# Decoder layer on one core: the first four attention steps between single products of the last two down tiles instead of behind whole tiles from the seventh on

## The reference

```python
x = x + attn(layernorm(x))            # 16 query heads, 2 key heads, head size 32, RoPE, causal
x = x + mamba(ctx, layernorm(x))      # state-space block: 16 states, a scan over 512 positions, gated by z
x = x + moe_ffn(layernorm(x))         # gate/up/down with DFF = 1408, 8 LoRA experts, the best 2 used
```

## Time and profile before

| what | value |
|---|---|
| median of 3 runs | 1439.26 us |
| the profiled execution's own time | 1439.63 us |
| its span | 1437.8 us |
| PE busy | 1290.9 us, 90% |
| DVE busy | 1026.8 us, 71% |
| ACT busy | 676.2 us, 47% |
| mean granted TensorE clock | 0.93 |

### The profile page before, as it was taken

One profiled execution on the slowest core, in us unless ns is written; L12 is line 12 of the kernel. 1 busy time (PEld: TensorE's weight loads), 2 busy tenths in 40 slices (PEclk: granted clock), 3 DMA queues, 4 the chain that ended last, 5 costly groups with the idle time before them and its releaser, 6 DMA issues.

```text
span 1437.8 us, 15860 instructions
## 1 busy us (share of the span) xinstructions
PE 1290.9 (90%) x5680; PEld 627.8 (44%) x5680; DVE 1026.8 (71%) x1238; ACT 676.2 (47%) x1465; POOL 89.0 (6%) x116
## 2 busy tenths in 40 slices
PE   5767778899998899899999799899999799799999
PEld 2334444444443465444444365444444365344443
DVE  5799996889899565789999574788899564521110
ACT  5356553365552395465543286365552287121110
POOL 0000001100000000010000000100000000100000
PEclk8856558999999899999999899999999899799999
DMA  6276662147777410147777410137777311011111
GB/s 233 56 179 152 149 136 56 46 126 186 186 198 170 118 31 1 45 112 186 186 196 168 106 44 20 45 91 188 186 188 178 83 58 31 15 38 55 55 59 54
DMA packets 53196, 158.50 MB, mean 110 GB/s; under 512 B 4992, under 2 KB 10880, under 8 KB 44672
## 3 DMA queue, kind: packets, MB, share of 16 engines
q0 software_dynamic: 9216, 67.11, 23.4%
q1 hardware_dynamic: 25520, 54.01, 11.4%
q10 hardware_dynamic: 18384, 36.37, 8.6%
HBM read 85.91 MB, written 4.46 MB: 63 GB/s over the span
## 4 chain that ended last, share of the span: by engine, by line
PE 61%; DVE 25%; ACT 7%; issue 4%; DMA 2%; ACTq 0%; POOL 0%; DVEq 0%
PE ps_a L920 20%; PE ps_a L934 10%; DVE state L1129 9%; PE ps_a L1005 6%; PE ps_b L945 5%; DVE state L1124 4%; PE ps_w L899 4%; PE ps_a L836 3%; ACT r L618 3%; DVE state L1134 3%; PE ps_b L853 2%; DVE neg_max L1165 2%; PE ps_a L968 2%; PE ps_w L868 2%; DMA y_sb<-state 1%
## 5 line engine op out<-in xcount | busy, mean ns | idle before, releaser
L920 PE MATMUL ps_a<-xt,w_sb 128*128 128x512 f32 x704 | 311.7, 595 | 0.0
L1129 DVE TENSOR_TENSOR_SCAN state<-decay,state 128x2048 f32<-128x2048 f32 (+1 forms) x82 | 284.4, 3478 | 2.5 <-ACT decay L584 0.6
L920 PEld LDWEIGHTS ps_a<-xt,w_sb 128*128 128x128 f32 x704 | 133.2, 191 | 170.0 <-issue 170.0
L682 ACT ACTIVATE r<-ps_a 128x512 f32<-128x512 f32 x132 | 78.5, 597 | 255.2 <-PE ps_a L934 139.1
L1307 DVE TENSOR_TENSOR r<-r,ps_a 128x512 f32<-128x512 f32 x132 | 90.0, 684 | 135.6 <-ACT r L682 135.6
L934 PE MATMUL ps_a<-r,wb_sb 128*128 128x512 f32 x352 | 165.6, 593 | 6.5 <-DVE r L1307 6.5
L584 ACT ACTIVATE decay<-dt_sb,decay_rate 128x511 f32<-128x511 f32 x256 | 163.0, 710 | 5.6 <-DVE state L1129 5.2
L618 ACT ACTIVATE r<-ps_a,neg_max 128x384 f32<-128x384 f32 (+3 forms) x224 | 121.6, 562 | 62.9 <-DVE neg_max L1165 56.8
L1134 DVE TENSOR_TENSOR state<-state,bc_sb 128x2048 f32<-128x2048 f32 (+1 forms) x73 | 147.6, 2022 | 1.6
L1124 DVE TENSOR_TENSOR state<-du_sb,bc_sb 128x2048 f32<-128x2048 f32 x64 | 146.2, 2284 | 1.5 <-DMA bc_sb<-bc_rows 0.9
L853 PE MATMUL ps_b<-cst,r 128*128 128x128 f32 x640 | 108.4, 307 | 25.8 <-ACT r L630 11.5
(11 more groups left out here) (137 smaller groups left out, 1419.5 us busy)
## 6 DMA issues: line engine op xcount, KB each, us to landing
y_sb<-state POOLq DMA_DIRECT2D x64, 1024.0 KB, 9.3
bc_sb<-bc_rows ACTq DMA_DIRECT2D x64, 512.0 KB, 5.9
w_sb<-in_w_tiles SPq DMA_DIRECT2D x44, 512.0 KB, 8.6
w_sb<-in_w_down SPq DMA_DIRECT2D x28, 256.0 KB, 4.2
wb_sb<-in_w_adapt SPq DMA_DIRECT2D x44, 128.0 KB, 2.1
xa<-in_x SPq DMA_DIRECT2D x4, 1024.0 KB, 5.4
wd_sb<-in_w_down SPq DMA_DIRECT2D x16, 256.0 KB, 7.3
out_x<-xb SPq DMA_DIRECT2D x16, 256.0 KB, 2.0
```

Source lines behind the costliest of these rows:

```text
L920: mm = nc.tensor.matmul(ps_a[:, 2 * (f % 2) + half, :], w_sb[:, slot, at + k * P:at + (k + 1) * P], xt[:, k, :], start=(k == 0), stop=Fals ...
L1129: done(nc.vector.tensor_tensor_scan(flat, decay[:, n % 2, tiles, :].rearrange("p j l -> p (j l)"), flat, 0.0, ALU.mult, ALU.add))
```

## The change

The early steps leave their places behind whole tiles. On PE they stand in a table `EARLY_AT` with places (f, i), "behind product i of tile f". Scores 0 come behind product 1 of tile 9, scores 1 behind product 2; in tile 10 transposes 0 stand behind product 1, transposes 1 behind product 2, scores 2 behind product 3; scores 3 stand behind the first closing product (place (FT, 0)). Tiles 7 and 8 follow tile 6 with nothing between. ACT does exponents 0 and 1 in slot 7, both moves in slot 8, exponents 2 and 3 in slots 9 and 10. DVE does maxima 0 and 1 in slot 7, behind that slot's scan piece, the inverses of 0 and 1 in slot 8 behind its piece, maxima 2 and 3 in slots 9 and 10; the inverse of 2 goes behind the residual additions, ahead of maxima 4. In batch 0 PE's order stays the same; those of ACT and DVE change as in the others.

```diff
-SCORES_AT = {FT - 5: 0, FT - 4: 1, FT - 2: 2, FT - 1: 3}
-TURNS_AT = {FT - 3: 0, FT - 2: 1}
+EARLY_AT = {(FT - 2, 1): ("scores", 0), (FT - 2, 2): ("scores", 1), (FT - 1, 1): ("turn", 0), (FT - 1, 2): ("turn", 1),
+            (FT - 1, 3): ("scores", 2), (FT, 0): ("scores", 3)}
...
             def early_steps(b, f):
-                if f in TURNS_AT:
-                    move_transposed(b, TURNS_AT[f])
-                if f in SCORES_AT:
-                    exponents(b, SCORES_AT[f])
+                if f == FT - 4:
+                    exponents(b, 0)
+                    exponents(b, 1)
+                elif f == FT - 3:
+                    move_transposed(b, 0)
+                    move_transposed(b, 1)
+                elif f >= FT - 2:
+                    exponents(b, f - FT + 4)
...
-            def early_steps(b, f):
-                if f in TURNS_AT:
-                    transpose_probs(b, TURNS_AT[f])
-                if f in SCORES_AT:
-                    scores(b, SCORES_AT[f])
+            def early_steps(b, place):
+                kind, s = EARLY_AT.get(place, (None, None))
+                if kind == "scores":
+                    scores(b, s)
+                elif kind == "turn":
+                    transpose_probs(b, s)
...
                         mm = nc.tensor.matmul(ps_a[:, i, :], hb[:, f, i * P:(i + 1) * P], wd_ring[slot],
                                               start=(f == 0), stop=False, skip_group_check=True)
+                        if b is not None and i < NT - 1:
+                            early_steps(b, (f, i))
                     mm.then_inc(wd_used, 1)
                     if b is not None:
+                        early_steps(b, (f, NT - 1))
                         project(b, f)
-                        early_steps(b, f)
                 pe.wait_ge(down_ready, t + 1)
                 for i in range(NT):
                     nc.tensor.matmul(ps_a[:, i, :], down_low[:, i * P:(i + 1) * P], bd_sb[:],
                                      start=False, stop=True, skip_group_check=True).then_inc(out_full, 1)
+                    if b is not None:
+                        early_steps(b, (FT, i))
...
                 project(0, f)
-                early_steps(0, f)
+            for place in EARLY_AT:
+                early_steps(0, place)
...
             def early_steps(b, f):
-                if f in SCORES_AT:
-                    s = SCORES_AT[f]
-                    maxima(b, s)
-                    if s >= 1:
-                        invert_sums(b, s - 1)
+                if f == FT - 4:
+                    maxima(b, 0)
+                    maxima(b, 1)
+                elif f == FT - 3:
+                    invert_sums(b, 0)
+                    invert_sums(b, 1)
+                elif f >= FT - 2:
+                    maxima(b, f - FT + 4)
...
                 for s in range(STEPS + 4):
+                    if s == EARLY:
+                        invert_sums(b, s - 2)
                     if EARLY <= s < STEPS:
                         maxima(b, s)
```

## The result

The changed kernel took 1405.37 us (median of 4, 1403.74 to 1408.29) for 1439.05 before (4 runs measured beside it); the ratio is 0.9768 with a 95% interval of 0.9748 to 0.9788. Two more sets of runs gave 0.9781 (0.9766 to 0.9795) and 0.9784 (0.9770 to 0.9799); one run of the kernel before beside the last set took 1570.17 us at a granted clock of 0.81 and is left out of it. The forecast was 1407.4 us, range 1404 to 1413. The profiled execution took 1406.83 us, its span was 1405.0.

A forecast was written before the change was run, and what follows sets the result against it. PE was taken as the bound (61% of the chain, 90% busy), DVE in batch 0; 30.7 us from batches 1 to 3 plus 1.3 from batch 0 made 32.0, giving 1407.4 us, range 1404 to 1413.

The forecast's parts named there:

- The wait: PE ahead of scores 0, batches 1 to 3: about 7.7 us idle each goes, values there 0.84 us earlier.
- The slow clock: Scores 0 and tile 7 after PE's rest: they return to full speed, 2.33 us gained in the second batch.
- The sum of batches 1 to 3: Down stages: idle plus slow clock gone, 10.07, 10.6 and 10.0 us, together 30.7, all kept through attention.
- Rival 4: Scores 0 to scores 4: mixing small products and transposes with full ones drops the clock to 1.2 GHz; 1443.7 us, chance 0.03.
- The rule on transpose passes: Transposes 0 and 1 inside tile 10: transpose passes don't count as busy, so the clock could fall; no size given.
- The cover: PE's later early steps: inputs ready ahead of need, 2.1 us at transposes 0, 2.3 at transposes 1, 2.2 at scores 3.
- Batch 0: DVE-bound: the `mul` of slot 7 fills 1.31 us idle ahead of maxima 0; gain 1.3 us, between 0 and 1.5.
- each addition lands within 11.1 us: Additions of states to y: landing 11.1 us after issue at most, so DVE's earlier `mul` pieces would not wait.

The follow-up runs named there:

- experiment 6: The changed kernel with all its early places on PE one tile (four products) earlier: 1420.92 us, ratio 0.9867 to the kernel before.
- Experiment 5: The kernel before, with PE doing eight surplus products while it waits for the value copy in batches 1 to 3: 1431.63 us, ratio 0.9953.
- Experiment 4: The changed kernel with its early steps behind whole tiles, the last two, and scores 3 behind the first closing product: 1408.36 us, ratio 0.9790.

## Why the prediction was right

**The wait.** The prediction said that the values are there 0.84 us before PE comes to scores 0 and that the wait is gone. This held in all three batches: scores 0 stand without idle time ahead of them, 0.9 us after the copy's end. The slack of 0.84 was tested by experiment 6: one tile (3.43) earlier gave a wait of 2.59, the difference to 0.01 us.

**The slow clock**, 7.5 us of the sum, was put down to the rest. Experiment 5 took away the rest and left the delay, and 6.8 us went by the medians; by the traces 2.26 + 2.81 + 2.20 = 7.3 us in the three batches, 2.26 in the second for the 2.33 computed.

**The sum of batches 1 to 3.** From value transposes to scores 4: 31.40, 31.95 (789.86 to 821.81) and 31.34 (1118.77 to 1150.11) before; 21.33, 21.33 (777.57 to 798.90) and 21.34 (1095.72 to 1117.06) after. Together 30.69 us, forecast 30.7. It stayed gained: attention shifted with scores 4. Rival 4, a clock that falls in the mix, did not come: the window over 470 to 482.3 us, with transposes 0 and 1 inside, has a granted clock of 1.00. The rule on transpose passes that the Trainium skill states (TensorE: Matmul & The Clock Gate, Part 4: PE-mode transpose) did not decide the time here; between full products the trace shows no effect of it.

**The cover.** None of the waits at transposes 0, transposes 1, scores 2 or scores 3 appears. Experiment 4 shows what their cover is worth: without a product between the two transposes PE waits 0.35 us and loses 0.54.

**Batch 0** was forecast at 1.3 us, "between 0 (another wait comes last) and 1.5". The mechanism held up to inverse 3 (90.71 to 87.20, less 1.99 of the start: 1.52). Up to batch 1's value transposes 0.27 and 0.29 us were left in two profiles and 1.77 in a third, and up to the end of the program 0.1 to 0.4. So this term was too high. Two things took the gain: the wait for an addition in two of the three profiles, and a slow clock in the passage to the feed-forward block, which the prediction did not look at. The argument that each addition lands within 11.1 us was made for one addition, not for a chain of them in which each is issued when the one before has landed and the next `mul` waits. The rows for that were in the profile before: in batch 0's attention the additions are issued every 9.4 to 12.2 us, 11.0 on average, and two of them are released by the landing of the one before. The waits of POOL in batch 0 before, and in the first profile of the changed kernel:

```profile
POOL y_sb L499 <- DMA y_sb<-state: 20.2, 2, 10.2
```
```profile
POOL y_sb L499 <- DMA y_sb<-state: 31.0, 3, 10.9
```

**What was not foreseen** is the variable start. The span of the first profile fell by 32.8 us: 30.69 in the three down stages, 0.27 in batch 0 and 1.99 at the start make 32.95, and the stages between and behind them took 0.15 longer. 32.0 was forecast. Without the 2.0 us of the start, which are chance, the fall would have been 30.8. The medians of the changed kernel, 1405.37, 1408.41 and 1406.45 us, lie on both sides of the forecast 1407.4. That the total came out so close is partly luck, that of the three batches is not.

## What to carry to other kernels

Ask of every in-order engine what stands behind a waiting instruction and doesn't need what it waits for: here two and a half tiles of products covered a wait of 7.7 us, with no instruction added. Count TensorE's idle time at more than its length: 7.7 us idle cost 10.1 and 2.6 us cost 4.3, while the 0.87 us of experiment 5 brought no slow rows. Place a chain of short dependent steps with one independent product between each two; that was worth a twentieth of the gain here, while lateness gave the rest. When a bound engine is made faster, follow the chains of transfers whose period is close to its own. And read a gain of a microsecond to the end of the program before you count it: here 1.6 us of one stretch were gone in the next and half back at the end.

## What the runs showed of the hardware

After a rest of 2.59 us PE ran on at full speed for 1.5 us, with a granted clock of 1.00, and then slowly for about 3 us: in experiment 6 the clock fell after the work had come back, so the slow rows are not the ones next to the idle time. The window that holds them has a granted clock of 0.91, for 1.00 in the changed kernel over the same 470 to 488 us:

```profile
470.00:488.00 18.00, 17.40 (x58) 7.67 (x58) 9.18 (x12) 4.44 (x20) 0.88 (x1) 0.91 0.34 76
```

After 7.7 us of rest the slow rows follow at once; there the clock had fallen during the rest (0.63 over 464 to 472 us before). Four instructions behind the same idle of 1.67 us ran in 1.95 to 1.96 us in some passages and in 2.95 to 3.65 in others, of one and the same kernel too. Eight surplus products in PE's wait cost nothing and won 2.2 to 2.8 us a batch. And half the bytes did not halve an addition: in batch 0 its time from issue to landing was 4.6 / 7.2 / 8.8 us (shortest, median, longest) with 512 KB in the changed kernel, for 7.0 / 9.6 / 11.1 with 1 MB.
